# Distances and layer 3's logits in four row groups of TensorE, layer 3's masks copied into PSUM, and new instruction orders

## The reference

```python
# layer 0: 8 heads of 16; adj is both edge weight and mask
scores = q @ k.T / 4 + adj * W_e[h];  scores = where(adj, scores, -inf)
x = layernorm(x + (softmax(scores) @ v) @ W_o.T)
# layer 1: convolutions of width 1 and 17, a message pass, a gated unit
s = x @ w_se.T + b_se                           # 3 numbers per node
A = exp(-(sq_i + sq_j - 2 * s_i . s_j)) * adj   # sq = sum(s * s)
x_in = concat([conv(x), A @ relu(x @ w_msg.T + b_msg)])
x = layernorm(x + gru(x_in, x))
# layer 2: h = x @ W_w.T + W_b;  u = adj * exp(e_i + f_j + a_b)
x = layernorm(x + (u / sum(u)) @ h)
# layer 3: 4 heads of 32
e = leaky_relu(e_i + e_j, 0.2);  e = where(adj > 0, e, -9e15)
x = layernorm(x + softmax(e) @ h)
```

## Time and profile before

| | |
|---|---|
| median of 3 runs | 1428.95 us (1428.47 to 1429.69) |
| the profiled execution | 1432.08 us, of which span in the profile 1430.3 us |
| TensorE busy | 1352.1 us (95% of the span) |
| TensorE weight loads busy | 1075.1 us (75%) |
| DVE busy | 1191.3 us (83%) |
| ACT busy | 1188.4 us (83%) |
| POOL busy | 663.1 us (46%) |
| chain that ended last, by engine | PE 78%, DVE 10%, POOL 5%, issue 4%, ACT 3% |
| granted clock of TensorE, mean | 0.976 |

### The profile page before, as it was taken

The page is one execution under the profiler, slowest core; times in us unless marked ns, Lnnn a source line. Parts: engine busy times, 40 slices in busy tenths (PEclk is TensorE's granted clock), DMA queues, the critical chain, the costliest instruction groups (busy, mean ns, idle before and its releaser), DMA issues.

```text
span 1430.3 us, 40514 instructions
## 1 busy us (share of the span) xinstructions
PE 1352.1 (95%) x13178; PEld 1075.1 (75%) x13267; DVE 1191.3 (83%) x3407; ACT 1188.4 (83%) x4353; POOL 663.1 (46%) x1014
## 2 busy tenths in 40 slices
PE   4799999999999999999999999999999999999964
PEld 3577788877778887777888777788877778887642
DVE  6568888888888888888888888888888888886763
ACT  3867888889888888998888899888889988887654
POOL 1133445554444555444455544445554444555532
PEclk7899999999999999999999999999999999999986
DMA  3100110011111001111100111111011111100000
GB/s 117 38 31 31 31 31 17 16 39 38 39 38 39 25 16 39 38 38 39 39 29 12 39 39 38 38 39 34 6 39 39 38 39 38 33 8 16 9 15 23
DMA packets 23825, 46.86 MB, mean 33 GB/s; under 512 B 2753, under 2 KB 2754, under 8 KB 23490
## 3 DMA queue, kind: packets, MB, share of 16 engines
q1 hardware_dynamic: 23618, 44.27, 9.8%
HBM read 35.88 MB, written 8.39 MB: 31 GB/s over the span
## 4 chain that ended last, share of the span: by engine, by line
PE 78%; DVE 10%; POOL 5%; issue 4%; ACT 3%; DVEq 0%; POOLq 0%; ACTq 0%
PE B L591 18%; PE B L689 14%; PE B L499 12%; PE B L537 5%; PE B L558 4%; DVE B L1353 4%; DVE x L1326 3%; POOL rstd L376 3%; PE B L808 2%; PE B L523 2%; PE B L788 2%; PE B L754 2%; PE B L581 2%; PE B L665 2%; PE B L683 2%
## 5 line engine op out<-in xcount | busy, mean ns | idle before, releaser
L995 ACT ACTIVATE e<-B,nm 128x128 f32<-128x128 f32 x1024 | 363.9, 385 | 12.5 <-DVE nm L1361 12.0
L499 PEld LDWEIGHTS B<-ident,e 128*128 128x128 f32 x1536 | 187.0, 144 | 104.3 <-issue 75.7
L499 PE MATMUL B<-ident,e 128*128 128x128 f32 x1536 | 230.0, 281 | 9.2 <-ACT e L1151 3.9
L995 ACT ACTIVATION_READ_ACCUMULATOR e<-B,nm 128x1 f32 x1024 | 231.9, 226 | 0.0
L1353 DVE SCALAR_TENSOR_TENSOR B<-an,rowb,mask 128x512 f32<-128x512 f32 x256 | 194.2, 794 | 19.0 <-ACT pT L1004 9.5
L1151 ACT ACTIVATE e<-l,nm 128x128 f32<-128x128 f32 x512 | 198.9, 400 | 10.0 <-DVE nm L1582 9.9
L1361 DVE TENSOR_REDUCE nm<-B 128x4 f32<-128x512 f32 x256 | 166.5, 683 | 35.0 <-PE B L537 34.8
L1004 ACT ACTIVATE pT<-B 128x512 f32<-128x512 f32 x256 | 157.9, 617 | 44.5 <-PE B L499 41.3
L373 POOL TENSOR_TENSOR veps<-meanv,eps 128x4 f32<-128x4 f32 x128 | 41.8, 326 | 328.9 <-DVE meanv L1320 328.8
L376 POOL TENSOR_TENSOR rstd<-veps,neghalf 128x4 f32<-128x4 f32 x128 | 139.7, 1092 | 10.0
L1582 DVE TENSOR_REDUCE nm<-l 128x4 f32<-128x512 f32 x128 | 87.0, 679 | 41.9 <-ACT l L1141 41.9
(11 more groups left out here) (201 smaller groups left out, 3471.1 us busy)
## 6 DMA issues: line engine op xcount, KB each, us to landing
xt<-in_x_t SPq DMA_DIRECT2D x32, 256.0 KB, 3.1
an<-in_adj_n SPq DMA_DIRECT2D x32, 256.0 KB, 2.7
xn<-in_x_n SPq DMA_DIRECT2D x32, 256.0 KB, 3.3
at<-in_adj_t SPq DMA_DIRECT2D x32, 256.0 KB, 3.2
out_x<-xo SPq DMA_DIRECT2D x32, 256.0 KB, 3.5
wm<-in_mats SPq DMA_DIRECT2D x1, 1088.0 KB, 9.4
wm<-in_mats SPq DMA_DIRECT2D x1, 832.0 KB, 7.1
wm<-in_mats SPq DMA_DIRECT2D x1, 320.0 KB, 3.0
```

The source lines that it names most:

```text
L499: last = mm(g(dst, b), g(src, b), ident[:, :], is_transpose=True, start=(b == 0), stop=True, skip_group_check=True)
L995: last = fn(g(e0[:, h % 2, :], b), g(bank, b), ACT.Exp, bias=nm0[:, h % 4, b:b + 1], accum_out=sum0[s % 2][:, b, head(h):head(h) + 1])
```

## The change

Distances: lr shrinks to 128 x 128 and is written by one instruction over all rows; TensorE issues four matmuls, one for each graph, each from the 32 rows of its graph (tile rows 32b to 32b + 31) into 128 columns of a bank of its own; ACT exponentiates in four instructions of 128 columns.

Logits: DVE copies each graph's mask, repeated for four heads, from bf16 into a PSUM bank (seed_mask3, new); POOL writes eim once, 128 columns for all graphs; TensorE issues the four graphs' matmuls together, each from its 32 rows, 512 columns, added onto the mask in its bank. The identity matmuls with the mask are gone.

Orders: every engine's step(t) is written out anew, with other banks and other group offsets. The offsets are larger by about 30 throughout (37 to 46 in place of 8 to 16, and STEPS with them), which changes nothing by itself, since steps without a live group issue nothing.

```diff
-        src_t = sb("src_t", [128, GB])
+        src_t = sb("src_t", [128, 1])
-        lr = sb("lr", [128, W])
+        lr = sb("lr", [128, N])
-        eim = sb("eim", [128, GB, N], BF16)
+        eim = sb("eim", [128, N], BF16)
@@ SP, step
                 load_xt(t)
+                load_at(t - 2)
                 load_an(t)
                 load_xn(t)
-                store(t - 8)
-                load_at(t - 1)
+                store(t - 10)
@@ POOL, split_ej
-                for b in range(GB):
-                    last = pool.tensor_scalar(eim[:, b, :], ejw[:, :], src_t[:, b:b + 1], src_i[:, b:b + 1], ALU.mult, ALU.add)
-                last.then_inc(q["ej_split"], 1)
+                pool.tensor_scalar(eim[:, :], ejw[:, :], src_t[:, :], src_i[:, :], ALU.mult, ALU.add)\
+                    .then_inc(q["ej_split"], 1)
@@ TensorE
-                mm(bank[:, :], ll[:, :], lr[:, :], start=True, stop=True).then_inc(q["arg_ps"], 1)
+                for b in range(GB):
+                    k = slice(32 * b, 32 * b + 32)
+                    last = mm(banks[b][:, 0:N], ll[k, :], lr[k, :], start=True, stop=True)
+                last.then_inc(q["arg_ps"], 1)
@@
-            def logits3(s, b, bank, users):
+            def logits3(s, banks):
 
                 if not live(s):
                     return
-                freed(pe, s, users)
-                pe.wait_ge(q["mask3_ready"], s + 1)
-                mm(bank[:, :], identb[:, :], g(mask3[s % 3], b).unsqueeze(1).broadcast_to([128, H3, N]),
-                   start=True, stop=False)
+                pe.wait_ge(q["seed3_done"], GB * s + GB)
                 pe.wait_ge(q["ej_split"], s + 1)
-                mm(bank[:, :], eim[:, b, :], ejm[:, :, :], start=False, stop=True).then_inc(q["e3_ps"], 1)
+                for b in range(GB):
+                    k = slice(32 * b, 32 * b + 32)
+                    last = mm(banks[b][:, :], eim[k, :], ejm[k, :, :], start=False, stop=True, skip_group_check=True)
+                last.then_inc(q["e3_ps"], GB)
@@ ACT, affinity
-                fn(aT[:, :], bank[:, :], ACT.Exp).then_inc(q["em_ready"], 1)
+                for b in range(GB):
+                    last = fn(g(aT, b), banks[b][:, 0:N], ACT.Exp)
+                last.then_inc(q["em_ready"], 1)
@@ DVE, sides
-                for b in range(GB):
-                    k = slice(32 * b, 32 * b + KS)
-                    v.scalar_tensor_tensor(out=lr[k, b * N:(b + 1) * N], in0=dd[k, :], scalar=sel[k, 0:1], in1=sqr[k, :],
-                                           op0=ALU.mult, op1=ALU.subtract)
+                v.scalar_tensor_tensor(out=lr[:, :], in0=dd[:, :], scalar=sel[:, 0:1], in1=sqr[:, :],
+                                       op0=ALU.mult, op1=ALU.subtract)
@@ DVE, new
+            def seed_mask3(s, b, bank, users):
+
+                if not live(s):
+                    return
+                freed(dve, s, users)
+                dve.wait_ge(q["mask3_ready"], s + 1)
+                v.tensor_copy(per(bank[:, :]), g(mask3[s % 3], b).unsqueeze(1).broadcast_to([128, H3, N]))\
+                    .then_inc(q["seed3_done"], 1)
@@ DVE, edge_mask3
-                wait(dve, q["e3_ps"], GB * (s - 2))
+                wait(dve, q["seed3_done"], GB * (s - 2))
@@ TensorE, step (58 calls before, 55 after; one shown)
-                logits3(t - 14, 3, B[1], (("nmT_ready", 2, 1, 1), ("hb_done", 1, 1, 1),
...
+                logits3(t - 42, (B[3], B[6], B[0], B[4]))
...
```

More of the change, by code:

```diff
@@ L1057, in message_relu, with affinity @@
                 fn(msg[:, :], msg[:, :], ACT.Relu).then_inc(q["msg_ready"], 1)
-            def affinity(s, bank):
+            def affinity(s, banks):
                 if not live(s):
@@ L1169, in step @@
             def step(t):
-                keep_d(t - 11, B[4])
-                exps(t - 9, 0, B[5])
-                keep_ej(t - 13, B[2])
-                squares(t - 11)
-                keep_probs3(t - 14, 2, B[7])
-                exps(t - 9, 1, B[3])
-                keep_probs(t - 9, 0, B[7])
-                exps(t - 9, 2, B[0])
-                keep_probs(t - 9, 1, B[6])
-                exps(t - 9, 3, B[1])
-                affinity(t - 11, B[2])
-                keep_probs3(t - 14, 3, B[6])
@@ L1195, in step @@
-                keep_probs(t - 9, 3, B[0])
-                tanh_r(t - 11, B[3])
-                exps(t - 9, 5, B[2])
-                keep_v(t - 9, B[0])
-                exps(t - 9, 6, B[4])
-                keep_probs(t - 9, 4, B[5])
-                tanh_z(t - 11, B[3])
-                keep_probs3(t - 13, 0, B[2])
-                exps(t - 9, 7, B[7])
-                keep_h3(t - 13, B[0])
-                keep_probs(t - 9, 5, B[1])
-                keep_probs3(t - 13, 1, B[5])
-                keep_k(t - 8, 0, B[2])
@@ L1208, in step @@
[L1208 to L1218 removed]
+                conv_relu(t - 42, B[6])
+                keep_probs3(t - 44, 0, B[5])
@@ new lines, in step @@
+                keep_q(t - 39, B[0])
+                leaky(t - 44, 3, B[4])
+                keep_gathered(t - 42, B[2])
+                keep_probs(t - 40, 7, B[5])
+                tanh_r(t - 42, B[3])
+                exps3(t - 44, 2)
+                exps(t - 39, 0, B[6])
+                exps(t - 39, 1, B[4])
+                tanh_z(t - 42, B[0])
+                keep_sums(t - 40, B[3])
+                exps(t - 39, 2, B[1])
+                keep_probs(t - 39, 0, B[7])
+                keep_v(t - 39, B[0])
@@ new lines, in step @@
+                keep_probs3(t - 44, 1, B[3])
+                exps3(t - 44, 3)
+                keep_x1(t - 41, B[5])
+                keep_h3(t - 44, B[3])
+                keep_probs(t - 39, 1, B[7])
+                exps(t - 39, 3, B[2])
+                keep_probs(t - 39, 2, B[0])
+                tanh_n(t - 42, B[1])
+                conv_input(t - 41, B[7])
+                keep_probs3(t - 44, 2, B[0])
+                keep_x3(t - 43, B[2])
+                keep_probs3(t - 44, 3, B[7])
+                exps(t - 39, 4, B[6])
@@ new lines, in step @@
+                keep_ej(t - 43, B[2])
+                keep_out3(t - 44, B[7])
+                keep_d(t - 41, B[1])
+                keep_probs(t - 39, 3, B[0])
+                exps(t - 39, 5, B[3])
+                squares(t - 41)
+                exps(t - 39, 6, B[4])
+                keep_probs(t - 39, 4, B[0])
+                keep_probs(t - 39, 5, B[2])
+                exps(t - 39, 7, B[5])
+                message_relu(t - 41)
+                leaky(t - 43, 0, B[3])
+                leaky(t - 43, 1, B[6])
@@ L1220, in _ @@
+                keep_probs(t - 39, 6, B[2])
+                keep_k(t - 38, 1, B[3])
+                keep_k(t - 38, 0, B[3])
+                exps3(t - 43, 0)
+                leaky(t - 43, 2, B[0])
+                exp_edges(t - 42)
+                affinity(t - 41, (B[3], B[7], B[5], B[2]))
+                exps3(t - 43, 1)
             act.wait_ge(q["parity_set"], 2)
@@ new lines, in step @@
+                stats1(t - 41, B[1])
+                edge_mask3(t - 39)
+                shared_to_phases(t - 40, B[7])
+                aggr1(t - 41)
+                row_max3(t - 42, 0)
+                shared_to_halves(t - 40, B[7], B[6], (("l3_done", -2, 4, 2), ("exp_done", 2, 8, 5),
+                    ("exp_done", 2, 8, 1), ("xc_ready", -1, 1, 1)))
+                stats0(t - 39)
+                hidden_bias(t - 41, (B[2], B[5]))
+                row_max3(t - 42, 1)
+                norm3(t - 44)
@@ new lines, in step @@
+                residual2(t - 41, (B[0], B[7]))
+                aggr0(t - 39)
+                row_max(t - 37, 0, B[6])
+                row_max(t - 37, 1, B[4])
+                invert_sums(t - 38)
+                row_max(t - 37, 2, B[1])
+                stats2(t - 41)
+                aggr2(t - 41)
+                norm0(t - 39)
+                residual3(t - 43)
+                row_max3(t - 42, 3)
+                seed_edges(t - 37, 4, B[6], (("exp_done", 0, 8, 1), ("xc_ready", -3, 1, 1),
+                    ("l3_done", -5, 4, 2), ("exp_done", -1, 8, 5)))
@@ L1697, in _ @@
+                row_max(t - 37, 3, B[2])
+                divide(t - 38, B[5])
+                half_tanh(t - 40)
             for t in range(STEPS):
```

443 lines of the change are left out of this document (205 added, 238 removed).

## The result

The changed kernel takes 1418.1 us (median of 4 runs, 1416.8 to 1419.3), the kernel before in the same comparison 1429.0: a ratio of 0.992, 95% interval 0.991 to 0.994, so 10.9 us faster. The forecast was 1395 us, 34 us faster. The direction was right, the size was off by two thirds.

The account below looks back on a forecast made before the run. TensorE's own work bounds the kernel: 29.9 us off over 26 periods, 3.3 in filling and draining, about 1 in the drain's waits, in all -34 from 1432.08; corrected for the profiled execution, 1395 us, 8-in-10 range 1378 to 1430.

Parts of the forecast that it names:

- What bounds the kernel: Steady part: TensorE's own work sets the period, busy 41.12 of 41.61 us; DVE has 4.85 us of slack, ACT 4.62.
- what is removed: TensorE, per group: old distances 0.86 us and four pairs of mask and logits 1.72 us, together 2.58 us off.
- what the new operations cost: TensorE, per group: new logits 0.55 us and new distances 0.55 us; DVE's four mask copies 2.64 us.
- POOL's shorter chain in the drain: POOL drops three instructions, so its chain ends 1.33 us sooner; TensorE's waits in the drain get shorter, two of 1.33.
- The store: SP issues it behind the loads; costed at nothing, up to 1 us a group kept for the range.
- 0.38 us more: TensorE, per group: the new order splits old runs, so changes of shape cost 1.23 us instead of 0.85.
- The price of a visit to 32 columns: TensorE: entering and leaving the 32-column shape was priced at 0.19 us on top of the work.
- 0.2 of new waits: TensorE, steady part: waits for seeds and similar add 0.2 us a period, taking 40.3 to 40.5 us.
- TensorE is busy only about half of the time: Filling and draining, the remaining six periods: only half of the 1.10 us gain counts, 3.3 us in all.
- Hidden while DVE's slack can shrink to 2.3: DVE, per group: net 1.28 us more work, 38.0 us in all, stays hidden if slack shrinks from 4.85 us.
- the cover is thinner: Rival: DVE keeps 3.2 of its 4.85 us of waits, period 41.2 us, total 1413 us; chance 0.20.
- 40.5: Steady part: forecast period in us a group, against 41.65 before; over 26 periods 29.9 us less.

Follow-up runs that it names:

- e1: Changed kernel with the second half of a graph's values moved right behind its first half on TensorE; 1435.8 us.
- e2: Kernel before with the second half of the values moved behind the third layer 3 transpose, one more split; 1442.7 us.
- e7: Changed kernel with the first half of the values moved later on TensorE, right ahead of the second half; 1420.9 us.
- e11: Changed kernel with one extra DVE row maximum a group whose result nobody reads; 1434.3 us.
- e8: Changed kernel with the logits moved between the convolution's halves, aggr1 ahead of shared_to_phases, and the values joined later; 1422.0 us.
- e15: Changed kernel with values joined later, logits inside the convolution, and calls reordered on DVE and ACT, including divide and shared_to_halves earlier; 1412.3 us.
- e5: Changed kernel's orders on all engines, with the old mask, logits and distance operations put back in their new places; 1478.6 us.

## Why the prediction was wrong

- *What bounds the kernel, what is removed, what the new operations cost.* Right: 2.58 us off, 1.1 on; copies of 686 ns where 660 were taken; POOL's shorter chain in the drain. The store was costed at nothing and cost 2.2 us in two groups, by the waits of norm3 that the prediction names as a sign of being wrong.
- *The term "0.38 us more" for split runs* failed. Counted on the timeline of the changed kernel the longer pieces add about 0.73, 0.35 more than costed: 26 x 0.35 = 9 us. The price of a visit to 32 columns was mis-sized: 0.33 us in e1 and e2 and 0.29 in e7, not 0.19, because three pieces get longer, the one ahead of the visit by 0.09, the last one in it by 0.10 to 0.12 and the one behind it by 0.05 to 0.10. I had counted two. In the changed kernel the three visits to columns cost 0.90 where 0.57 was taken, the two visits to rows 0.77 where 0.66 was taken; the two runs of before cost about 0.1 more than the 0.85 taken, which gives some of it back.
- *The term "0.2 of new waits"* failed. There were about 0.55 a group behind the logits, 0.35 more than costed, 9 us. project_k behind logits3 was named as a queue to watch, but for the seeds; that it writes the bank which leaky must have read was not. project_k could start 0.8 us behind the start of the logits (0.32 for the set, one short group of 0.44 and 0.05 for the shape), and the chain that it waits for takes 1.1 us (the logits at 738.39 to the end of leaky at 739.5).
- *"TensorE is busy only about half of the time"* in filling and draining was a misreading: outside the 26 groups it is busy 282 of 347.5 us in the kernel before, 81%, and of the 40 slices of the span only the first two and the last two lie under 90%. The term of 3.3 us rests on it, so that the 4.3 us for this part came out at 4.2 is luck.
- *"Hidden while DVE's slack can shrink to 2.3"* was the wrong kind of argument. DVE kept 3.6 us of idle time in the changed kernel, yet an instruction of 0.61 us cost 0.56 (e11). Total idle time isn't room; room is what lies between the last point where an engine is released by another and the instruction that the other waits for. It didn't decide this result, since TensorE's own stack was 0.05 us longer, but in e7 and e8 it shows as the wait of x1_T for divide, 0.25 and 0.24 us.
- *The rival "the cover is thinner"* (41.2 us a group, 1413 us) came nearest, in part by luck: it has DVE setting the period, while about half of the difference came from shapes.

In short, 40.5 was reachable with these operations (e15), but not with the orders of the change; that e15 has the very number of the forecast is luck too, since it saves a visit that the forecast paid for. What remains open: which part of e5's 1.45 us comes from splits and which from the old operations standing in an order not made for them; and why project_k and hidden2 hold longer in e15.

## What to carry to other kernels

Price a split run by both neighbours and the last piece of each visit, from a row where such a visit stands alone. In a kernel whose order is written by hand, look at each wait of the bounding engine for what the other engine does just ahead of the awaited instruction, and whether it could come first; an engine with 3.6 us idle a period may still have none to give. And keep the order for the first steps apart from that of the steady part: here it was worth 11 us.
